# A load order, a moved norm and a new order of the first rows in a two-batch transformer kernel

## The chip, the cores and the metric

The kernel runs on one core of one Trainium2 chip. A core has a matrix engine (TensorE, PE in the profile; its weight loads are PEld), a vector engine (VectorE, DVE), a scalar engine (ScalarE, ACT), GpSimd (POOL) and SyncE (SP), which here issues nearly all DMAs. Each engine works through its own instructions in the order written and waits on semaphores. The metric is the device time of one execution in microseconds (us); lower is better.

## The reference

Two layers on x of 2 batches x 2048 rows x 512 features, all in float32. The part that matters here is the first: x is normalised, goes through single-head causal self-attention, and is added and normalised again. What follows (cross-attention to 77 context rows, a small MLP, a feed-forward layer of width 2048 with dequantised weights) isn't touched.

```python
def _layernorm(x, axis=-1, eps=1e-05):
    m = jnp.mean(x, axis=axis, keepdims=True)
    v = jnp.var(x, axis=axis, keepdims=True)
    return (x - m) / jnp.sqrt(v + eps)
...
    def self_attn(x, Wq, Wk, Wv):
        Q, K, V = (x @ Wq, x @ Wk, x @ Wv)
        energy = jnp.einsum('bqd,bkd->bqk', Q, K)
        lengths = jnp.sum(energy[:, 0] != 0, axis=-1)
...
        energy = jnp.where(pad | causal, NEG_INF, energy)
        score = jax.nn.softmax(energy / np.sqrt(DK), axis=-1)
        return jnp.einsum('bqk,bkd->bqd', score, V)
...
    z = self_attn(x, Wq1, Wk1, Wv1)
    x = layer_norm(x + z, ln1_g, ln1_b)
...
x = x + jnp.tanh(g_xattn[0]) * _L0_xattn_ref(_layernorm(x, axis=-1), ctx_1024, ...)
```

## The kernel before

**Precision.** Every product is made of three passes on float32 values split into a high and a low half (`PASSES`). So each result that feeds another product is read out of its bank (PSUM) twice: ScalarE copies the high half (`hi`, L1009) and VectorE subtracts it to get the low half (`lo`, L1494). A product of four chunks is 12 matmuls (`product`, L643). Turns (transposes) by PE are at L653 and L687, those of the attention's probabilities at L777.

**Stages.** A prologue (0 to about 65 us) turns and joins the weights. Then each batch has an x stage and an attention stage; batch 0 ends and batch 1 starts at about 365 to 405 us; the attention of batch 1 ends at about 730 us. The rest of the 1749 us isn't touched.

**The x stage** goes over 16 tiles of 128 rows. For tile t: SP loads it into one of four places (`load_xa`, L397; place t % 4 is free when tile t-4 has been normed), VectorE makes mean and variance (`stats_x`, L1528 and L1530), GpSimd the reciprocal root (`rstd_x`, L1330 and L1332), VectorE the norm (`norm_x`, L1553) into one of two places, PE turns it (`turn_x`, L653), ScalarE and VectorE split it (`hi_x`, `lo_x`) into xT, PE multiplies it with the value weights (`values`), and these are split too (`hi_v`, `lo_v`). VectorE also makes the dot of the normed tile with the first query (`dot_x`, L1571), whose non-zero results are the key count. PE's order is values(t-2), turn_x(t), values(t-1), turn_x(t+1) and so on. Tiles 0 to 2 are done ahead: in batch 0 in the prologue, in batch 1 inside the last row of batch 0's attention.

**The attention stage** goes over 16 rows i of 128 queries; row i has i // 4 + 1 chunks of keys. Its order is written out by hand in `attention_order`, as triples (kind, i, c), and every engine walks the same list and does its own part of each entry:

- S: scores of row i, chunk c (PE; VectorE masks them and takes the maximum, L1658 and L1668). X: exponentials (ScalarE, L1077).
- T: turn the probabilities (PE L777, ScalarE hi, VectorE lo). V: product with the values (PE).
- Q: a chunk of the next four rows' queries (PE, hi, lo).
- A: the end of a row, first part: VectorE norms that row's x again, divides and adds (L1681 to L1686), makes statistics (L1528, L1530); GpSimd makes the root, and then `make_xo(i + 2)` (L1351), a sum with the loaded rows of x that waits for their DMA. B: second part, VectorE scales and shifts (L1534, L1536); then SP stores the row (L495) and loads the x of row i + 2 (`load_x`, L471), and stores what `make_xo` made (L475).
- In the last row of batch 0 (15): L statistics, M norm, N turn and split of tiles 0 to 3 of batch 1, W the split of the value weights, D the product for the first query. VectorE's norm of tile 0 of batch 1 goes into the place from which `make_xo` reads a bias row (`b3_row`), so it waits until the last `make_xo` of batch 0 is made.

**SP's queue** is one list in order. In batch 0's prologue the loads of tiles 0 to 3 and of the value weights are followed by two stores (g_scratch 640 KB, v_scratch 616 KB, L464 and L466) which wait for the last product of the prologue, and then by the loads of tiles 4 and on. Between the batches the first four tiles of batch 1 are asked for after the last store of `make_xo`'s results; they lie where the scores of even rows lie (`Srow`), so they wait until row 14's probabilities are turned.

**Before the first scores** PE makes queries(0, m) for four chunks m, with the one-column product that counts the keys (L758) ahead of chunk 2. VectorE makes all four low halves, then reads the count (L1632), builds the padding mask (L1638 to L1644), and only then releases the banks for scores. PE waits for all four low halves before row 0's scores.

## Time and profile before

| what | value |
|---|---|
| time, median of 3 runs | 1750.45 us (1750.41 to 1756.3) |
| profiled execution, its own time | 1750.76 us |
| its span, first to last instruction | 1749.0 us |
| PE busy | 1667.6 us (95%) |
| VectorE busy | 847.7 us (48%) |
| ScalarE busy | 550.6 us (31%) |
| GpSimd busy | 359.5 us (21%) |
| chain that ended last: PE, VectorE, ScalarE, DMA, GpSimd, issue | 82%, 8%, 2%, 2%, 2%, 2% |
| mean granted TensorE clock | 0.981 of full speed |

The profile is one execution, taken by the hardware profiler. A share of busy time is an average over stages with different limits, so the stages that the change touches have to be read one by one: where an engine sat idle, for how long, and what released it. Matmuls are pipelined and their ends are modelled, so rows of PE may overlap by some tenths of a microsecond. TensorE's clock is granted at one of two levels, 1.2 or 2.4 GHz; 1.00 in a window means all of it at 2.4, 0.5 all of it at 1.2. Times in the rows are from the start of the span.

### The profile page before, as it was taken

The page shows a single profiled execution, that of the slowest core. Times are in us where ns is not written, and L with a number is a line of the kernel's source. Part 1 is how long each engine was busy: PE and PEld are TensorE (multiplying, and loading weights), DVE is VectorE, ACT ScalarE, POOL GpSimd, SP SyncE. Part 2 cuts the span into 40 slices and gives each one's busy share as a digit, 9 for nine tenths or more (in the row PEclk, how much of TensorE's full clock was granted, in tenths as well). Part 3 has the DMA queues.
Part 4 walks back from the last instruction along what each step waited for, and adds up shares of the span by engine and source line. Part 5 has one row for each costly group of instructions (what it writes and reads, how often), then busy time and mean ns, then how long its engine had stood idle before and what let it go on. Part 6 is the DMA issues. An engine that isn't in the chain of part 4 may idle for free.

```text
span 1749.0 us, 20563 instructions
## 1 busy us (share of the span) xinstructions
PE 1667.6 (95%) x7734; PEld 1355.9 (78%) x7734; DVE 847.7 (48%) x1746; ACT 550.6 (31%) x964; POOL 359.5 (21%) x509
## 2 busy tenths in 40 slices
PE   6998999989999999889999799999999999999999
PEld 4777888866778888668778587878787887878787
DVE  4576653448564534578788765322323223232311
ACT  3222211112211212266656534222223223232222
POOL 0121110112121100078888830100000000000000
PEclk9999999989999999799999899999999999999999
DMA  6211211122021101734544342101010101000000
GB/s 188 72 49 65 74 37 37 37 72 91 19 85 43 55 30 37 243 105 157 181 151 150 126 134 84 61 0 49 1 49 0 49 0 49 1 26 23 6 20 24
DMA packets 68822, 117.22 MB, mean 67 GB/s; under 512 B 11201, under 2 KB 13249, under 8 KB 68571
## 3 DMA queue, kind: packets, MB, share of 16 engines
q1 hardware_dynamic: 64968, 110.12, 19.1%
q10 hardware_dynamic: 3757, 5.80, 1.1%
q8 instruction: 62, 1.02, 0.2%
q14 instruction: 35, 0.29, 0.1%
HBM read 81.05 MB, written 34.84 MB: 66 GB/s over the span
## 4 chain that ended last, share of the span: by engine, by line
PE 82%; DVE 8%; ACT 2%; DMA 2%; POOL 2%; issue 2%; SPq 0%; ACTq 0%; DVEq 0%; POOLq 0%
PE banks L643 77%; PE banks L653 3%; PE banks L777 2%; DMA plain<-in_x 1%; DVE split_q L1494 1%; ACT split_q L1009 1%; DVE plain L1997 1%; ACT split L1009 1%; DVE split L1962 1%; DVE split L1494 1%; DVE plain L2040 1%; DVE small L1528 1%; DMA plain<-in_L_xattn_Wq 1%; DMA plain<-in_L_xattn_fc_w 0%; DVE plain L1571 0%
## 5 line engine op out<-in xcount | busy, mean ns | idle before, releaser
L643 PE MATMUL banks<-split_q,split 128*128 128x512 f32 x2328 | 576.8, 397 | 5.6 <-POOL split L1387 4.5
L643 PE MATMUL banks<-split 128*128 128x512 f32 (+4 forms) x2292 | 551.5, 391 | 28.3 <-DVE split L1494 16.0
L643 PEld LDWEIGHTS banks<-split 128*128 128x128 f32 (+3 forms) x2292 | 417.3, 188 | 131.8 <-issue 22.8
L643 PEld LDWEIGHTS banks<-split_q,split 128*128 128x128 f32 x2328 | 434.6, 190 | 99.2 <-POOL split L1387 6.1
L643 PE MATMUL banks<-split,split_q 128*128 128x512 f32 (+2 forms) x1728 | 396.0, 382 | 5.2 <-DVE small L1632 3.5
L643 PEld LDWEIGHTS banks<-split,split_q 128*128 128x128 f32 x1728 | 307.6, 190 | 61.5 <-DVE split_q L1494 4.3
L1494 DVE TENSOR_TENSOR split<-banks,split 128x512 fp32r<-128x512 f32 (+5 forms) x232 | 146.8, 641 | 173.3 <-ACT split L1009 172.7
L1009 ACT ACTIVATE split<-banks 128x512 fp32r<-128x512 f32 (+5 forms) x232 | 125.8, 557 | 323.9 <-PE banks L777 198.4
L1962 DVE TENSOR_TENSOR split<-plain,split 128x512 fp32r<-128x512 f32 x128 | 88.3, 690 | 256.5 <-ACT split L1300 256.4
L1294 ACT ACTIVATE plain<-banks,small 128x512 f32<-128x512 f32 x128 | 87.7, 685 | 285.9 <-PE banks L643 285.9
L1494 DVE TENSOR_TENSOR split_q<-banks,split_q 128x512 fp32r<-128x512 f32 x68 | 46.8, 688 | 254.4 <-ACT split_q L1009 254.4
L1009 ACT ACTIVATE split_q<-banks 128x512 fp32r<-128x512 f32 x68 | 40.5, 598 | 298.8 <-PE banks L653 205.2
L643 PE MATMUL banks<-split_x,split 128*128 128x512 f32 x444 | 109.1, 394 | 3.5 <-DVE split L1962 3.5
L1413 POOL TENSOR_TENSOR small<-small 128x4 f32<-128x4 f32 x8 | 2.1, 264 | 498.5 <-DVE small L1981 498.5
L643 PEld LDWEIGHTS banks<-split_x,split 128*128 128x128 f32 x444 | 82.2, 188 | 25.6 <-DVE split L1962 8.8
L1351 POOL TENSOR_TENSOR plain<-plain 128x512 f32<-128x512 f32 x32 | 41.2, 1288 | 287.5 <-DMA plain<-in_x 283.1
L653 PE MATMUL banks<-ident,plain 128*128 128x128 f32 x432 | 69.6, 295 | 29.0 <-DMA plain<-in_L_xattn_Wq 11.2
L653 PEld LDWEIGHTS banks<-ident,plain 128*128 128x128 f32 x432 | 54.7, 151 | 48.2 <-DVE plain L1553 15.6
L1300 ACT ACTIVATE split<-plain 128x512 fp32r<-128x512 f32 x128 | 81.0, 633 | 4.1
L1330 POOL TENSOR_TENSOR small<-small 128x1 f32<-128x1 f32 x64 | 18.4, 287 | 294.5 <-DVE small L1530 294.1
L1077 ACT ACTIVATE plain<-plain,small 128x128 f32<-128x128 f32 (+15 forms) x32 | 38.6, 1206 | 111.6 <-DVE small L1674 111.6
L1658 DVE CUSTOM_DVE_ANT_0 plain<-banks,plain 128x512 f32<-128x512 f32 (+2 forms) x72 | 43.4, 602 | 59.4 <-PE banks L643 58.5
(151 smaller groups left out, 1244.4 us busy)
## 6 DMA issues: line engine op xcount, KB each, us to landing
...
```

Source lines behind the costliest of these rows:

```text
L643: mm = nc.tensor.matmul(out, left(c, l), right(c, r), start=start and c == 0 and (l, r) == PASSES[0], stop=stop and c == chunks - 1 and (l ...
L653: mm = nc.tensor.transpose(bank[:, c * P:(c + 1) * P], block_of(c), ident[:])
L777: mm = nc.tensor.transpose(PS[:, 2 + n % 2, j * P:(j + 1) * P], Srow[:, i % 2, lo:lo + P], ident[:])
L1009: nc.scalar.activation(dst, src, copy).then_inc(sems[1], inc)
L1077: nc.scalar.activation(Srow[:, i % 2, 0:w], Srow[:, i % 2, 0:w], ACT.Exp, bias=nb[:, i % 2:i % 2 + 1], scale=SCALE, accum_out=rowsum[:, i ...
L1294: nc.scalar.activation(HF3[:, f % 2], PS[:, f % 2], ACT.Silu, bias=b1f[:, f:f + 1]).then_inc(hf3_ready, 1)
L1300: nc.scalar.activation(hid3[f % 2][:, 0, :], HF3[:, f % 2], copy).then_inc(f_hi, 1)
L1330: nc.gpsimd.tensor_tensor(out, var, eps_col, ALU.add).then_inc(eps_added, 1)
L1351: nc.gpsimd.tensor_tensor(x_shifted, xin[:, i % 2], b3_row, ALU.add).then_inc(xo_made, 1)
L1494: nc.vector.tensor_tensor(dst, src, hi_part.bitcast(F32), ALU.subtract).then_inc(sems[1], inc)
L1658: return nc.vector.tensor_tensor_reduce(out=row[:, at + lo_:at + lo_ + n], in0=src, in1=pad[:, at + lo_:at + lo_ + n], scale=1.0, scalar=- ...
L1962: nc.vector.tensor_tensor(hid3[f % 2][:, 1, :], HF3[:, f % 2], hid3[f % 2][:, 0, :].bitcast(F32), ALU.subtract).then_inc(f_lo, 1)
```

## The change

1. **Loads, batch 0.** SP asks for tiles 4, 5 and 6 right behind the value weights, each when tile t-4 is normed, ahead of the two stores. The later loop begins at tile 7.
2. **Loads, batch 1.** The first four tiles are asked for one row earlier (at i = 13, before the wait for row 13's end), tiles 4 to 6 at i = 15, before the wait for row 15's end. The value weights stay at i = 14.
3. **Norm of tiles 3 to 15.** It leaves VectorE. ScalarE makes it as an Identity with a scale (the reciprocal root) and a bias, minus mean times root; GpSimd makes the bias with two more operations on one column. In ScalarE's order it stands ahead of `hi_v(t - 2)`. It waits for the bias, the turn of tile t-2, the dot of tile t-2 and the norm of tile t-1.
4. **Before the first scores.** VectorE reads the count after two of the four low halves and spreads the rest over the mask's making. PE's first scores wait chunk by chunk (`first_score`).
5. **Order of rows 0 to 3.** Row 0's A is parted into Z (norm and add) and E (statistics, root, `make_xo`); Z comes ahead of row 2's turn, E and B behind it; B of row 0 is now behind V of row 2, B of row 1 behind Q's chunk 2, and row 3's exponentials behind row 2's turn.

```diff
@@ -89,9 +89,9 @@
 
 
     order = [("S", 0, 0), ("X", 0, 0), ("S", 1, 0), ("X", 1, 0), ("T", 0, 0), ("S", 2, 0), ("X", 2, 0), ("V", 0, 0),
-             ("T", 1, 0), ("S", 3, 0), ("X", 3, 0), ("A", 0, 0), ("V", 1, 0), ("B", 0, 0), ("T", 2, 0), ("Q", 1, 0),
-             ("A", 1, 0), ("V", 2, 0), ("Q", 1, 1), ("B", 1, 0), ("Q", 1, 2), ("A", 2, 0), ("Q", 1, 3), ("B", 2, 0),
-             ("T", 3, 0), ("S", 4, 0), ("S", 4, 1), ("X", 4, 0), ("V", 3, 0)]
+             ("T", 1, 0), ("S", 3, 0), ("Z", 0, 0), ("V", 1, 0), ("T", 2, 0), ("X", 3, 0), ("E", 0, 0), ("Q", 1, 0),
+             ("V", 2, 0), ("B", 0, 0), ("A", 1, 0), ("Q", 1, 1), ("Q", 1, 2), ("B", 1, 0), ("A", 2, 0), ("Q", 1, 3),
+             ("B", 2, 0), ("T", 3, 0), ("S", 4, 0), ("S", 4, 1), ("X", 4, 0), ("V", 3, 0)]
     for i in range(4, NB):
         n0 = chunks_of(i)
         n1 = chunks_of(i + 1) if i + 1 < NB else 0
...
@@ -153,7 +153,7 @@
     for b in range(B):
         order += [("x", b, t) for t in range(AHEAD + 2, NB)]
         for kind, i, c in ORDER:
-            if kind == "A":
+            if kind in ("A", "E"):
                 order.append(("z", b, i))
             elif kind == "L" and b + 1 < B:
                 order.append(("x", b + 1, c))
...
@@ -460,6 +461,9 @@
                              allow_slow_non_contiguous=True).then_inc(const_in, 16)
             sp.wait_ge(split_lo, C)
             weight("L0_xattn_Wv1", wv_raw[0], wv_in)
+            for t in range(4, 7):
+                sp.wait_ge(x_normed, t - 3)
+                load_xa(sp, 0, t)
             sp.wait_ge(mm_free, 2 + MM0)
             sp.dma_start(g_dram.rearrange("b p n -> p b n"),
                          g_0.rearrange("p b c h n -> p b (c h n)").bitcast(F32)).then_inc(parked, 16)
...
@@ -474,7 +478,7 @@
                     sp.wait_ge(xo_made, b * NB + i + 1)
                     sp.dma_start(xo_dram[b * S + i * P:b * S + (i + 1) * P, :], x_shifted).then_inc(xo_stored, 16)
 
-                for t in range(4, NB):
+                for t in range(7, NB):
                     sp.wait_ge(x_normed, b * NB + t - 3)
                     load_xa(sp, b, t)
                 load_x(0)
...
@@ -485,10 +489,15 @@
                 for i in range(NB):
                     if i + 1 < NB:
                         store_xo(i + 1)
-                    if i == NB - 2 and b + 1 < B:
+                    if i == NB - 3 and b + 1 < B:
                         sp.wait_ge(tp_full, TURNS["p", b, NB - 2, 3] + 1)
                         for t in range(4):
                             load_xa(sp, b + 1, t)
+                    if i == NB - 1 and b + 1 < B:
+                        for t in range(4, 7):
+                            sp.wait_ge(x_normed, (b + 1) * NB + t - 3)
+                            load_xa(sp, b + 1, t)
+                    if i == NB - 2 and b + 1 < B:
                         sp.wait_ge(s_full, (b + 1) * SS1)
                         weight("L0_xattn_Wv1", wv_raw[1], wv_in)
                     sp.wait_ge(x1_ready, b * NB + i + 1)
...
@@ -757,11 +766,10 @@
                         pe.wait_ge(counted, b + 1)
                         nc.tensor.matmul(PS[:, 0, 0:1], all_ones, keys_seen, start=True, stop=True).then_inc(s_full, 2)
                     queries(0, m)
-                pe.wait_ge(mm_free, b * MM1 + 2 + MM0 + NB + C)
 
                 for kind, i, c in ORDER:
                     if kind == "S":
-                        if i % 4 == 0 and c == 0 and i:
+                        if i % 4 == 0 and c == 0:
                             first_score(2 + T_BEFORE[i], i // 4, 0, width_of(i, 0))
                         else:
                             score(2 + T_BEFORE[i] + c, i % 4, c * 512, width_of(i, c))
...
@@ -1054,6 +1062,14 @@
                     "p (b n) -> p b n", b=B), sems=(mm_full, mm_hi))
 
 
+            def norm_x(b, t):
+                act.wait_ge(mean_scaled, 2 * (b * (NB - AHEAD - 1) + t - AHEAD))
+                act.wait_ge(tp_full, TURNS["x", b, t - 2, 0] + 1)
+                act.wait_ge(dotted, b * NB + t - 1)
+                act.wait_ge(x_normed, b * NB + t)
+                nc.scalar.activation(xn[:, t % 2], xa[:, t % 4], ACT.Identity, bias=nmr1[:, t:t + 1],
+                                     scale=rs1[:, t:t + 1]).then_inc(x_normed, 1)
+
             for b in range(B):
                 def hi_v(t):
                     hi(MM0 + t, V[t][:, 0, :], PS[:, 4 + t % 2], b, MM1, (mm_full, mm_hi))
...
@@ -1062,6 +1078,8 @@
                     hi(MM0 + NB + g * C + m, QT[:, m, 0, :], PS[:, 4 + m % 2], b, MM1, (mm_full, mm_hi))
 
                 for t in range(AHEAD, NB):
+                    if t > AHEAD:
+                        norm_x(b, t)
                     if t - AHEAD == 4:
                         act.wait_ge(parked, 32)
                     hi_v(t - AHEAD)
...
@@ -1333,6 +1352,14 @@
 
             def rstd_x(b, t):
                 rstd(NORMS["x", b, t], mv1[:, t, 1:2], rs1[:, t:t + 1])
+                if t > AHEAD:
+                    n = b * (NB - AHEAD - 1) + t - AHEAD
+                    pool.wait_ge(rstd_ready, NORMS["x", b, t] + 1)
+                    nc.gpsimd.tensor_tensor(nmr1[:, t:t + 1], mv1[:, t, 0:1], rs1[:, t:t + 1], ALU.mult).then_inc(
+                        mean_scaled, 1)
+                    pool.wait_ge(mean_scaled, 2 * n - 1)
+                    nc.gpsimd.tensor_tensor(nmr1[:, t:t + 1], zero_col, nmr1[:, t:t + 1], ALU.subtract).then_inc(
+                        mean_scaled, 1)
 
             for t in range(AHEAD + 2):
                 rstd_x(0, t)
...
@@ -1353,7 +1380,7 @@
                 make_xo(0)
                 make_xo(1)
                 for kind, i, c in ORDER:
-                    if kind == "A":
+                    if kind in ("A", "E"):
                         rstd(NORMS["z", b, i], mvE[:, i % 2, 1:2], rsE[:, i % 2:i % 2 + 1])
                         if i + 2 < NB:
                             make_xo(i + 2)
...
@@ -1615,8 +1642,6 @@
                 for t in range(AHEAD, NB + AHEAD):
                     if AHEAD + 2 <= t + 1 < NB:
                         stats_x(b, t + 1)
-                    if AHEAD + 1 <= t < NB:
-                        norm_x(b, t)
                     if AHEAD <= t - 1 < NB:
                         lo_x(b, t - 1)
                     lo_v(t - AHEAD)
...
@@ -1624,9 +1649,8 @@
                         dot_x(b, t - 1)
                 nc.vector.tensor_scalar(cnt16, row_0, 0.0, None, ALU.not_equal, ALU.add,
                                         accum_out=keys_seen).then_inc(counted, 1)
-                for m in range(C):
-                    lo_q(0, m)
-
+                lo_q(0, 0)
+                lo_q(0, 1)
                 dve.wait_ge(s_full, b * SS1 + 2)
                 for c in range(4):
                     ins = nc.vector.tensor_scalar(lnc[:, c:c + 1], PS[:, 0, 0:1], -512.0 * c, None, ALU.add)
...
@@ -1637,11 +1661,12 @@
                 for c in range(4):
                     last = p1.done(nc.vector.tensor_scalar(pad[:, c * 512:(c + 1) * 512], keys[:],
                                                            lnc[:, c:c + 1], -BIG, ALU.is_ge, ALU.mult))
+                lo_q(0, 2)
                 p1.wait(last)
-
                 p1.link(nc.vector.reciprocal(ln, lnc[:, 0:1]))
                 p1.link(nc.vector.tensor_scalar(ln, ln, 0.0, None, ALU.mult))
                 p1.link(nc.vector.tensor_scalar(pad, pad, ln, None, ALU.add))
+                lo_q(0, 3)
 
                 def scores(i, c):
                     k, w, at = 2 + T_BEFORE[i] + c, width_of(i, c), c * 512
...
@@ -1674,7 +1699,7 @@
                     nc.vector.tensor_scalar(nb[:, i % 2:i % 2 + 1], nmx[:, 0:1], -SCALE, None,
                                             ALU.mult).then_inc(mx_ready, 1)
 
-                def end_a(i):
+                def add_rows(i):
 
                     dve.wait_ge(x_in[i % 2], b * NB * 8 + (i // 2 + 1) * 16)
                     dve.wait_ge(xo_made, b * NB + i + 1)
...
@@ -1686,6 +1711,8 @@
                     nc.vector.scalar_tensor_tensor(out=U[:, i % 2], in0=PS[:, 6 + i % 2],
                                                    scalar=rcp[:, i % 2:i % 2 + 1], in1=xin[:, i % 2],
                                                    op0=ALU.mult, op1=ALU.add).then_inc(z_free, 1)
+
+                def stats_z(i):
                     dve.wait_ge(z_free, b * NB + 2 + i + 1)
                     statistics(p1, U[:, i % 2], mvE[:, i % 2], i + 1)
...
@@ -1703,7 +1730,12 @@
                         n, k, w = TURNS["p", b, i, c], T_BEFORE[i] + c, width_of(i, c)
                         lo(n, PT[k % 2][:, 1, 0:w], PS[:, 2 + n % 2, 0:w], PT[k % 2][:, 0, 0:w])
                     elif kind == "A":
-                        end_a(i)
+                        add_rows(i)
+                        stats_z(i)
+                    elif kind == "Z":
+                        add_rows(i)
+                    elif kind == "E":
+                        stats_z(i)
                     elif kind == "B":
                         end_b(i)
                     elif b + 1 < B and kind == "L":
...
```

In the `x` stage of batch 0, ScalarE's order (names: banks is PSUM, split is xT and V, plain is a float32 area with x as loaded, normed x and scores; L1009 and L1017 are `hi`, L1070 is the new norm). Before:

```order
L1009 ACTIVATE split<-banks 128x512
L1009 ACTIVATE split<-banks 128x4x128
L1009 ACTIVATE split<-banks 128x512
L1009 ACTIVATE split<-banks 128x4x128
L1009 ACTIVATE split<-banks 128x512
```

and after:

```order
L1017 ACTIVATE split<-banks 128x512
L1017 ACTIVATE split<-banks 128x4x128
L1070 ACTIVATE plain<-plain,small 128x512
L1017 ACTIVATE split<-banks 128x512
L1017 ACTIVATE split<-banks 128x4x128
L1070 ACTIVATE plain<-plain,small 128x512
```

A third operation per tile stands between the split of one tile and the values of the next.

SP's queue at the end of batch 0 (L471 and L475 load x of a row, L475 and L479 store what `make_xo` made, L397 and L398 load tiles of batch 1, L438 and L439 the value weights, L495 and L504 store a row). Before:

```order
L495 DMA x_scratch<-plain 128x512
L471 DMA plain<-in_x 128x512
L475 DMA xo_scratch<-plain 128x512
L397 DMA plain<-in_x 128x512 x4
L438 DMA raw<-in_L_xattn_Wv 128x4x512
L495 DMA x_scratch<-plain 128x512 x2
L397 DMA plain<-in_x 128x512 x12
```

and after:

```order
L398 DMA plain<-in_x 128x512 x4
L504 DMA x_scratch<-plain 128x512
L475 DMA plain<-in_x 128x512
L479 DMA xo_scratch<-plain 128x512
L439 DMA raw<-in_L_xattn_Wv 128x4x512
L504 DMA x_scratch<-plain 128x512
L398 DMA plain<-in_x 128x512 x3
L504 DMA x_scratch<-plain 128x512
L398 DMA plain<-in_x 128x512 x9
```

The four loads moved ahead of row 13's store, row 15's load and the store behind it, and three of the next twelve ahead of row 15's store.

VectorE's order in attention rows 0 to 2 of batch 0, from row 0's division and sum on (L1686 and L1711). Before:

```order
L1686 SCALAR_TENSOR_TENSOR plain<-banks,small,plain 128x512
L1528 BN_STATS small<-plain 128x6
L1530 BN_AGGR small<-small 128x2
L1534 SCALAR_TENSOR_TENSOR plain<-plain,small 128x512
L1536 SCALAR_TENSOR_TENSOR plain<-plain,small 128x512
L1494 TENSOR_TENSOR split<-banks,split 128x384
L1494 TENSOR_TENSOR split_q<-banks,split_q 128x512
```

and after:

```order
L1711 SCALAR_TENSOR_TENSOR plain<-banks,small,plain 128x512
L1521 TENSOR_TENSOR split<-banks,split 128x384
L1555 BN_STATS small<-plain 128x6
L1557 BN_AGGR small<-small 128x2
L1521 TENSOR_TENSOR split_q<-banks,split_q 128x512
L1561 SCALAR_TENSOR_TENSOR plain<-plain,small 128x512
L1563 SCALAR_TENSOR_TENSOR plain<-plain,small 128x512
```

The low half of row 2's turned probabilities (128x384) now comes right behind the sum, and row 0's end behind the first chunk of the next queries.

## Rows read from the trace of the kernel before

**Rows 1.** The page: busy us, share of the span, instructions

```profile
PE 1667.6 (95%) x7734; PEld 1355.9 (78%) x7734; DVE 847.7 (48%) x1746; ACT 550.6 (31%) x964; POOL 359.5 (21%) x509
```

**Rows 2.** Windows: stretch, us, busy of each engine (x instructions), clock, DMA, GB/s

```profile
70.00:80.00 10.00, 7.55 (x27) 6.19 (x28) 6.15 (x13) 1.68 (x3) 1.97 (x4) 0.66 0.28 88
```

**Rows 3.** Timeline of PE, batch 0: start, us, line, [idle before <- releaser]

```profile
72.45 1.12 PE L653 MATMUL banks<-ident,plain 128*128 128x128 f32 x4 [3.96 <-DVE plain L1553]
...
78.11 0.60 PE L653 MATMUL banks<-ident,plain 128*128 128x128 f32 x4
...
114.41 0.60 PE L653 MATMUL banks<-ident,plain 128*128 128x128 f32 x4
...
117.74 0.60 PE L653 MATMUL banks<-ident,plain 128*128 128x128 f32 x4
```

**Rows 4.** Timeline of all engines, the same place: VectorE

```profile
66.62 0.68 DVE L1571 SCALAR_TENSOR_TENSOR plain<-banks,plain 128x512 f32<-128x512 f32 x1
...
70.90 0.69 DVE L1528 BATCH_NORM_STATS2 small<-plain 128x6 f32<-128x512 f32 x1 [3.59 <-DMA plain<-in_x]
```

**Rows 5.** Timeline of all engines, one tile of batch 1's x stage

```profile
407.57 0.69 DVE L1494 TENSOR_TENSOR split<-banks,split 128x512 fp32r<-128x512 f32 x1 [0.43 <-ACT split L1009]
...
408.91 0.69 DVE L1528 BATCH_NORM_STATS2 small<-plain 128x6 f32<-128x512 f32 x1
...
409.85 0.55 DVE L1553 TENSOR_SCALAR plain<-plain,small 128x512 f32<-128x512 f32 x1
...
410.31 1.30 DVE L1494 TENSOR_TENSOR split<-banks,split 128x512 fp32r<-128x512 f32 x2
...
410.45 0.66 PE L653 MATMUL banks<-ident,plain 128*128 128x128 f32 x4 [0.20 <-DVE plain L1553]
```

**Rows 6.** Groups by form: ScalarE over the span, GpSimd at 75 to 118

```profile
L1171 ACT ACTIVATE plain<-plain,small 128x512 f32<-128x512 f32 x28 | 22.7, 812 | 16.0 <-DVE plain L1997 16.0
...
L1332 POOL TENSOR_TENSOR small<-small 128x1 f32<-128x1 f32 x11 | 6.0, 549 | 0.9
L1330 POOL TENSOR_TENSOR small<-small 128x1 f32<-128x1 f32 x11 | 4.5, 414 | 30.4 <-DVE small L1530 30.4
```

**Rows 7.** Timeline of all engines between the batches

```profile
358.93 0.49 PE L777 MATMUL banks<-ident,plain 128*128 128x128 f32 x3
...
367.47 1.09 ACT L1009 ACTIVATE split<-banks 128x512 fp32r<-128x512 f32 x2 [1.33 <-PE banks L777]
368.61 1.26 POOL L1351 TENSOR_TENSOR plain<-plain 128x512 f32<-128x512 f32 x1 [19.44 <-DMA plain<-in_x]
...
370.26 1.87 SPq L397 DMA_DIRECT2D plain<-in_x  x4
...
373.05 0.69 DVE L1528 BATCH_NORM_STATS2 small<-plain 128x6 f32<-128x512 f32 x1 [7.60 <-DMA plain<-in_x]
...
374.15 0.19 POOL L1330 TENSOR_TENSOR small<-small 128x1 f32<-128x1 f32 x1 [4.29 <-DVE small L1530]
...
375.70 5.46 PE L643 MATMUL banks<-split 128*128 128x512 f32 x12 [7.89 <-DVE split L1494]
```

**Rows 8.** Timeline of PE, batch 1's x stage: turns of tiles 3 and 14

```profile
403.27 0.66 PE L653 MATMUL banks<-ident,plain 128*128 128x128 f32 x4 [3.24 <-DVE plain L1553]
...
442.72 0.60 PE L653 MATMUL banks<-ident,plain 128*128 128x128 f32 x4
```

**Rows 9.** Timeline, attention rows 0 to 3; the last row is of batch 1

```profile
136.71 3.00 PE L643 MATMUL banks<-split,split_q 128*128 128x128 f32 x24 [1.77 <-DVE small L1632]
...
154.10 2.29 PE L643 MATMUL banks<-split 128*128 128x512 f32 x9 [2.88 <-DVE split L1494]
...
160.39 0.74 DVE L1534 SCALAR_TENSOR_TENSOR plain<-plain,small 128x512 f32<-128x512 f32 x1
...
169.55 2.98 PE L643 MATMUL banks<-split 128*128 128x512 f32 x12 [0.49 <-DVE split L1494]
...
483.05 3.51 PE L643 MATMUL banks<-split 128*128 128x512 f32 x9 [2.89 <-DVE split L1494]
```

4 lines of the change are left out of this document (3 added, 1 removed).

## The prediction

> **What bounds the kernel now.** I read the page's busy times first: TensorE (PE) is busy for 95% of the span [rows 1]. So what an edit to VectorE, ScalarE or a load is worth is only the time in which PE waits for them. The table by windows shows where that is in the part that the diff touches: at 70 to 80 us, for one, PE is busy for 7.55 of 10 us, with a granted clock of 0.66 [rows 2]. The timelines of these places give four kinds of loss:
>
> 1. At 68.49 to 72.45, in the first tiles of batch 0, PE waits 3.96 us for the norm of tile 3 [rows 3]. VectorE stands in front of it with the statistics of tile 4, which wait for their load until 70.90 [rows 4]: that load was queued on SP behind two large stores.
> 2. In the rest of the x stage two tiles take 7.18 us (403.27 to 410.45), 3.59 each [rows 5, 8], while PE alone needs 3.33 (114.41 to 117.74) [rows 3].
> 3. Between the batches PE waits 7.89 us (to 375.70), then runs 12 products in 5.46 us that elsewhere take 2.98, and waits again 3.24 us before 403.27 [rows 7 to 9].
> 4. In the first four rows of attention it waits 1.77, 2.88 and 0.49 us [rows 9].
>
> **The change part by part.**
>
> Early loads, batch 0. Tiles 4 to 6 are now asked for as soon as the norms of tiles 0 to 2 are made, ahead of the two stores. Tile 2 is normed before tile 3, so all three are there long before 70.90. VectorE can begin tile 4's statistics when the dot of tile 1 is done (66.62 + 0.76 = 67.4 [rows 4]). ScalarE's norm of tile 3 waits for the same dot and takes 0.81 us [rows 6], to 68.2; PE wants it at 68.49. The low half of tile 2 comes after the statistics (408.91 to 409.85 in [rows 5], 0.94) and ends at 69.1, so PE's next values start some 0.2 late. Tile 4's turn stood at 78.11 and should stand at 68.49 + 3.33 + 0.2 = 72.0: **6.1 us less**. 2.3 us of that is the slow clock after the wait (from 72.45 to 78.11 one tile took 5.66 us, not 3.33 [rows 3]).
>
> Norm on ScalarE. Before, one chain ran twice per pair of tiles: the product ends, ScalarE copies 0.6, VectorE makes the low half (407.57), the dot, the statistics, and the norm (409.85), and PE turns it at 410.45 [rows 5]. The norm leaves VectorE, 0.45 us from start to start of a neighbour. What replaces it: ScalarE waits for the dot (about 2.1 us after a product's end), norms in 0.81 [rows 6] and is ready at 2.95, while PE comes for it at 3.33: 0.4 us of slack. ScalarE's load rises to 0.6 + 0.6 + 0.81 = 2.0 of 3.33 us. GpSimd gets two one-column operations a tile. The nearest row is its add, 0.41 us on average here and 0.19 in the one at 374.15 [rows 6, 7]; with the power, 0.55 [rows 6], the bias is ready 1.3 to 2.1 us after the statistics, which run a tile ahead, so it comes before the dot or with it. Next late is VectorE's low half of x: 410.31 + 0.69 before, 0.45 earlier now, within 0.1 us of where PE wants it. So I take 3.36 us a tile. Batch 0, tiles 4 to 14: 36.30 us (78.11 to 114.41 [rows 3]) become 33.6, **2.7 less**. Batch 1, tiles 3 to 14: 39.45 (403.27 to 442.72 [rows 8]) become 37.0, **2.4 less**.
>
> One rule speaks on GpSimd's share. The row shows the add at 0.41 us on average in the x stage, where it starts within VectorE's norm, and 0.19 us where it starts beside a statistics instruction [rows 6, 7]. The Trainium skill, page "SBUF — State Buffer", section "Who interferes with whom", says that GpSimd and VectorE share one pair of ports, that a tensor_scalar of VectorE may take the pair whole, and that the other then blocks for the instruction. By that rule the three short operations cost 0.19 each once the norm has left VectorE, and the bias has 0.8 us of slack instead of none; the sum above is the same by either, the chance of the rival on ScalarE is not.
>
> Between the batches. The next batch's first four tiles are now loaded one row earlier. Their place in memory is free when row 14's last scores are turned, at 359.4; before, SP asked for them only at 370.26, because it stood behind row 13's store, the load of row 15 and the store that needs it [rows 7]. Of that step all moves: four loads; the weights stay where they were and are asked for at 370.3, 1.9 us earlier. VectorE comes free at 373.05 - 7.60 = 365.45 and makes two statistics by 367.3; ScalarE has row 15's first transposes evicted at 368.05 [rows 7], VectorE's low half ends at 368.7, and PE starts at 368.9 instead of 375.70: **6.8 less**. With a wait of 1.0 us in place of 7.89 the slow clock goes too: 5.46 - 2.98 [rows 7, 9], **2.5 less**. What is late next: the norm of tile 0 overwrites what GpSimd reads until 369.9 (368.61 + 1.26 [rows 7]), and GpSimd's roots follow, so it is made at 371.3, when PE is still in its first product (to 371.8). Two further waits of 0.2 to 0.3 us appear behind VectorE's row end, so **0.5 back**. Before 403.27 the second load wait goes (tiles 4 to 6 are asked for before row 15's store), but ScalarE's norm of tile 3 and the low half of tile 2 are still behind the dot: 3.24 us become about 1.0, **2.2 less**. Together 11.0.
>
> First groups. Counting the keys moves ahead of the last two low halves and the first scores may start on three of four chunks, so the 1.77 us become 0.4. Row 0's statistics and end move behind rows 2 and 3, so the third product, at 154.10 [rows 9], can start at about 149.7. But little of these 4.4 us survives. Row 1's end stood at 160.39 [rows 9]; now it is queued behind Q's third chunk, whose low half ends at 159.0: 1.4 us earlier. From there the chain is unchanged: SP's load of row 3, GpSimd's sum with it, the root of row 2, row 2's end, the low half, PE at 169.55. So the last product of the group starts **1.4 us earlier per batch**, 2.8 together, and PE waits some 2.2 us there in place of 0.49. Bounds: 0 (the chain starts no earlier) to 4.4 a batch (it binds nothing).
>
> Sum: 6.1 + 2.7 + 2.4 + 11.0 + 2.8 = 25.0. The profiled execution took 1750.76 us for a span of 1749.0; the median of the runs is 1750.45. **Forecast 1725.5 us.**
>
> **The rivals.**
> - *Clock.* In batch 1 the wait of 2.89 us was followed by 9 products in 3.51 us, in batch 0 the same wait by 9 in 2.29 [rows 9]. The new 2.2 us wait may draw the slow clock in either batch (1.2 us each and as much again behind it), or the old losses may go. The Trainium skill, "TensorE: Matmul & The Clock Gate", Part 1, says that the monitor runs freely, not from the wait's start; by that rule neither case can be read off the length of a wait, and the two rows agree. Price: minus 2 to plus 4.5, 1723 to 1730; inside the forecast's own range.
> - *First groups pay in full.* If row 1's end is not held by the chunk's low half, up to 3 us more a batch: 1719.5.
> - *A new wait between the batches.* VectorE does rows' ends and the next batch's tiles in one order; if tile 0's norm (held by GpSimd to 371.3) keeps PE from its second product, half of the 11.0 stays lost: 1731. If the loads come no earlier, since SP still waits somewhere before them (the change doesn't do what it says), all 11: 1736.5.
> - *ScalarE's chain leads, and the kernel gets slower.* The new norm stands ahead of the copy of the values on ScalarE. This closes a loop without PE: norm 0.81, copy 0.6, low half 0.6, dot 0.75, together 2.8 us a tile. It decides from 3.33. The other parts gain 19.9, so slower than before by 0.5% needs a loop of 3.59 + (19.9 + 8.8) / 23 = 4.8 us. That would take a table load (1.28 us each way) around each Identity: loop 5.4, time 1750.8 - 19.9 + 23 x 1.8 = 1772. Against it: Identity already runs beside Exp and Copy in the cross stage at 0.81 us [rows 6], and the built program still has three table loads.
> - A milder form: the bias or the dot comes 0.3 us late, and the pace stays at 3.59: 1730.6.
>
> **How the numbers follow.** Half a per cent (8.8 us) is about what a measurement of this kernel can tell from no change. Forecast with its clock cases, 1720 to 1730.5: 0.62. First groups in full, 1714 to 1720: 0.11. Pace unchanged or half of the gain between the batches lost, 1730.5 to 1735: 0.16. Loads no earlier, 1735 to 1741: 0.06. Within 0.5%: 0.02. Slower: 0.03. The range 1717 to 1734 leaves out less than 2 in 10. Faster 0.95.
>
> **What would show it.** Right: no wait at 68.49; turns in the x stage 3.33 to 3.4 us apart; SP's four loads of tiles at about 359; PE's first product of row 15 at 368.9 less the 10.2 us gained before it, in 3.0 us; in both first groups a wait of 2 us before the last product. Wrong: turns still 3.59 apart with ScalarE or GpSimd named as releaser; a wait over 2 us behind row 15's first product; the last product of a first group 4 us earlier, not 1.4. The sum is most exposed in the part between the batches, which carries 11 of 25 us on a chain that no row shows as a whole.

## The result, and the profile after

| | before | after |
|---|---|---|
| first measurement, median of 4 runs each | 1753.38 us (1750.41 to 1759.38) | 1726.08 us (1724.2 to 1726.23) |
| the same kernel after once more, beside 9 runs of before | 1752.96 us (1749.56 to 1757.45) | 1724.9 us (1723.93 to 1726.59) |
| profiled execution, span | 1749.0 us | 1724.2 us |

The ratio is 0.9838 with an interval of 0.9806 to 0.9869, and 0.9839 (0.982 to 0.9857) the second time: faster by 1.6%. The forecast was 1725.5 us, 25.0 less than before. The medians of the two comparisons differ by 27.3 and 28.1 us, the two profiled executions by 24.7 (24.8 of span). One execution, the profiled one of the experiment "Loads alone", ran throughout at a mean granted clock of 0.576 and took 2680.52 us; it stands in no number below.

The page of the changed kernel: span, busy us with share and instructions, and the chain that ended last.

```profile
span 1724.2 us, 20645 instructions
...
PE 1658.7 (96%) x7734; PEld 1351.6 (78%) x7734; DVE 836.8 (49%) x1720; ACT 570.2 (33%) x990; POOL 362.4 (21%) x562
...
PE 86%; DVE 6%; ACT 2%; POOL 2%; DMA 2%; issue 1%; ACTq 0%; SPq 0%; DVEq 0%
```

Against [rows 1] the 26 norms have gone from DVE to ACT (1746 to 1720 and 964 to 990 instructions), and POOL has its operations on one column. PE's busy time fell by 8.9 us with the same 7734 matmuls, which fits slow clock that went. The rest of the 24.8 us of span is idle time of PE.

Windows of the kernel after (us, busy of each engine, clock, DMA share, GB/s), the stretch of [rows 2]:

```profile
70.00:80.00 10.00, 10.00 (x50) 7.95 (x49) 7.90 (x19) 5.48 (x9) 3.37 (x12) 1.00 0.29 79
```

PE is busy for 10.00 instead of 7.55 us, with 50 matmuls instead of 27 and a granted clock of 1.00 instead of 0.66. The timeline of PE in batch 0's x stage, where [rows 3] had its turns (start us, us, line, idle before and releaser):

```profile
67.53 0.66 PE L662 MATMUL banks<-ident,plain 128*128 128x128 f32 x4
...
71.05 0.60 PE L662 MATMUL banks<-ident,plain 128*128 128x128 f32 x4
...
104.56 0.60 PE L662 MATMUL banks<-ident,plain 128*128 128x128 f32 x4
```

The turn of tile 3 has no wait. From tile 3's turn to tile 4's it is 3.52 us, one tile plus the 0.2 us of the late low half, and the ten tiles to 104.56 take 33.51 us, 3.35 each.

The timeline between the batches and at the end of batch 1's x stage (SPq is SP issuing a DMA), where [rows 7, 8] were:

```profile
348.86 1.76 SPq L398 DMA_DIRECT2D plain<-in_x  x4
```

```profile
358.35 2.98 PE L652 MATMUL banks<-split 128*128 128x512 f32 x12 [1.13 <-DVE split L1521]
...
365.21 0.63 PE L662 MATMUL banks<-ident,plain 128*128 128x128 f32 x4 [0.28 <-DVE split L1521]
...
381.25 0.66 PE L662 MATMUL banks<-ident,plain 128*128 128x128 f32 x4 [0.72 <-ACT plain L1070]
...
418.27 0.60 PE L662 MATMUL banks<-ident,plain 128*128 128x128 f32 x4
```

The wait of 7.89 us is 1.13, the product behind it takes 2.98 instead of 5.46, and the wait of 3.24 is 0.72. The eleven tiles take 37.02 us.

One tile of batch 1 on all engines, the counterpart of [rows 5]:

```profile
386.20 0.68 DVE L1598 SCALAR_TENSOR_TENSOR plain<-banks,plain 128x512 f32<-128x512 f32 x1
...
386.92 0.70 DVE L1555 BATCH_NORM_STATS2 small<-plain 128x6 f32<-128x512 f32 x1
387.06 0.82 ACT L1070 ACTIVATE plain<-plain,small 128x512 f32<-128x512 f32 x1 [1.01 <-DVE plain L1598]
...
387.86 0.66 DVE L1521 TENSOR_TENSOR split<-banks,split 128x512 fp32r<-128x512 f32 x1
...
387.97 0.62 PE L662 MATMUL banks<-ident,plain 128*128 128x128 f32 x4
388.02 0.19 POOL L1349 TENSOR_TENSOR small<-small 128x1 f32<-128x1 f32 x1 [2.48 <-DVE small L1557]
...
388.29 0.55 POOL L1351 TENSOR_TENSOR small<-small 128x1 f32<-128x1 f32 x1
...
388.92 0.19 POOL L1358 TENSOR_TENSOR plain<-small 128x1 f32<-128x1 f32 x1
```

The norm on ACT starts at the end of the dot (387.06) beside VectorE's statistics of the next tile, takes 0.82 us to 387.88, and PE turns its result at 387.97. GpSimd's add takes 0.19 us here, where [rows 6] had a mean of 0.41.

The first groups of attention, PE of batch 0 and then of batch 1:

```profile
113.69 1.52 PE L652 MATMUL banks<-split,split_q 128*128 128x512 f32 x6
...
139.50 2.20 PE L652 MATMUL banks<-split 128*128 128x512 f32 x9
...
152.95 2.27 PE L652 MATMUL banks<-split,split_q 128*128 128x512 f32 x15 [0.56 <-DVE split_q L1521]
...
157.40 4.58 PE L652 MATMUL banks<-split 128*128 128x512 f32 x12 [2.19 <-DVE split L1521]
...
161.80 0.61 PE L785 MATMUL banks<-ident,plain 128*128 128x128 f32 x4
...
427.57 1.75 PE L652 MATMUL banks<-split,split_q 128*128 128x512 f32 x7
...
471.33 4.54 PE L652 MATMUL banks<-split 128*128 128x512 f32 x12 [2.25 <-DVE split L1521]
```

The product of 9 has lost its wait of 2.88 us, and the last product of the group has a wait of 2.19 in place of 0.49 [rows 9]. Those 12 matmuls then take 4.58 and 4.54 us, not 2.98; the granted clock over them is 0.62 and 0.63 (157.40 to 161.90, 471.33 to 475.70). The same three places (first queries, last product, next turn) in the kernel before, of which [rows 9] has only the product: the queries of batch 0 and 1 and the turns behind the products.

```profile
123.65 1.52 PE L643 MATMUL banks<-split,split_q 128*128 128x512 f32 x6
...
172.37 0.60 PE L777 MATMUL banks<-ident,plain 128*128 128x128 f32 x4
...
451.99 1.30 PE L643 MATMUL banks<-split,split_q 128*128 128x512 f32 x5
...
502.88 0.60 PE L777 MATMUL banks<-ident,plain 128*128 128x128 f32 x4
```

From these and from [rows 3, 7 to 9] comes the account of the 24.8 us of span. Where 358.93 stood before, the same turns stand at 348.35; batch 1's last product started at 500.06 before, and the turn behind it stands at 475.68 after.

| stretch | before | after | gained | predicted |
|---|---|---|---|---|
| start to tile 2's turn (not touched) | 65.11 | 64.28 | 0.8 | 0 |
| to tile 4's turn | 13.00 | 6.77 | 6.2 | 6.1 |
| batch 0, tiles 4 to 14 | 36.30 | 33.51 | 2.8 | 2.7 |
| first queries to the last product of the group | 45.90 | 43.71 | 2.2 | 1.4 |
| that product, to the next turn | 2.82 | 4.40 | -1.6 | 0 |
| rest of batch 0's attention (172.37 to 358.93) | 186.56 | 186.55 | 0 | 0 |
| between the batches (358.93 to 403.27) | 44.34 | 32.90 | 11.4 | 11.0 |
| batch 1, tiles 3 to 14 | 39.45 | 37.02 | 2.4 | 2.4 |
| first queries to the last product, batch 1 | 48.07 | 43.76 | 4.3 | 1.4 |
| that product, to the next turn | 2.82 | 4.35 | -1.5 | 0 |
| all behind it (not touched) | 1246.1 | 1248.5 | -2.4 | 0 |

Tile 14's turn to the first queries gives 0.1 more. The last line is code that no edit touches, and it changes from one execution to the next: in the second measurement's profiled execution (1723.93 us) it took 1245.35 us, and over all the profiled executions here, "Loads alone" left out, 1245.3 to 1250.3.

### The profile page after: what moved, and what is told of

The parts are those of the page before. It is cut to its first block, busy times and chain, and to the rows that moved or that the text cites. A ratio compares the mean times of both kernels' runs of the same rounds, so it can differ in the third digit from the quotient of the medians.

```text
span 1724.2 us, 20645 instructions
## 1 busy us (share of the span) xinstructions
PE 1658.7 (96%) x7734; PEld 1351.6 (78%) x7734; DVE 836.8 (49%) x1720; ACT 570.2 (33%) x990; POOL 362.4 (21%) x562
## 3 DMA queue, kind: packets, MB, share of 16 engines
q8 instruction: 62, 1.02, 0.2%
## 4 chain that ended last, share of the span: by engine, by line
PE 86%; DVE 6%; ACT 2%; POOL 2%; DMA 2%; issue 1%; ACTq 0%; SPq 0%; DVEq 0%
PE banks L652 80%; PE banks L662 3%; PE banks L785 2%; DVE split_q L1521 1%; ACT split_q L1017 1%; DVE plain L2029 1%; DVE split L1994 1%; DVE plain L2072 1%; DVE split L1521 1%; DMA plain<-in_L_xattn_Wq 1%; DMA plain<-in_L_xattn_fc_w 1%; DMA plain<-in_x 0%; ACT split L1017 0%; POOL split L1414 0%; POOL plain L1426 0%
## 5 line engine op out<-in xcount | busy, mean ns | idle before, releaser
L1017 ACT ACTIVATE split<-banks 128x512 fp32r<-128x512 f32 (+5 forms) x232 | 124.7, 557 | 268.1 <-PE banks L785 207.6
L1017 ACT ACTIVATE split_q<-banks 128x512 fp32r<-128x512 f32 x68 | 40.5, 598 | 290.9 <-PE banks L662 205.4
L1378 POOL TENSOR_TENSOR plain<-plain 128x512 f32<-128x512 f32 x32 | 41.3, 1291 | 284.3 <-DMA plain<-in_x 279.8
L1349 POOL TENSOR_TENSOR small<-small 128x1 f32<-128x1 f32 x64 | 12.8, 199 | 263.7 <-DVE small L1557 263.1
```

What stands on the lines that cost most here:

```text
L1017: nc.scalar.activation(dst, src, copy).then_inc(sems[1], inc)
L1378: nc.gpsimd.tensor_tensor(x_shifted, xin[:, i % 2], b3_row, ALU.add).then_inc(xo_made, 1)
```

## Experiments

Each was timed beside runs of the kernel before (medians 1751.19, 1751.1 and 1752.96 us in the three sets). "Control" is the kernel after in the last set, 1724.9 us.

### One part of the change at a time

**Loads alone**: only the edits to SP's order (points 1 and 2 of the change) in the kernel before.

> The kernel before with the new load order of SP alone (parts 1 and 2 of the change). My theory, by the sum of the prediction: batch 0 loses its wait of 3.96 us for the first tile but keeps VectorE's norm behind the statistics, so 5.5 us less with the slow clock; between the batches the 7.89 us wait, the slow clock and the 3.24 us wait go, 11 us less; the pace of the x stage stays at 3.59 us a tile. Together 16.5 us, 1734. Rival (the loads only work together with the norm on ScalarE, because VectorE's one order is what holds the tiles): the waits before tile 3's turn stay near 3 us and the gain is under 10 us, above 1740.

Measured: 1735.9 us (1734.07 to 1739.9, three runs), ratio 0.9903 (0.9873 to 0.9932). That is 15.3 us less, the size that was expected, and the interval leaves out the rival's "under 10 us". Where in the kernel these 15.3 us fall, no trace shows.

**Norm alone**: only point 3.

> The kernel before with the norm of tiles 3 to 15 on ScalarE and its bias on GpSimd alone (part 3). My theory: the pace of the x stage falls from 3.59 to 3.36 us a tile, which is 5.1 us less over both batches, and the load waits stay (VectorE's low half of tile 2 still stands behind tile 4's statistics): 1745. GpSimd's add falls from 0.41 to 0.19 us in the x stage. Rival (without early loads ScalarE's chain, not VectorE's, sets the pace): pace 3.59 or more, 1750 or above.

Measured: 1745.93 us (1743.12 to 1749.96, eight runs), ratio 0.9963 (0.9947 to 0.9979), 5.3 us less. PE at tile 3 of batch 0:

```profile
71.41 5.49 PE L644 MATMUL banks<-split_q,split 128*128 128x512 f32 x12 [3.60 <-DVE split L1515]
```

The turn of tile 3 has no wait any more, but the wait went to the product behind it, with the slow clock, because VectorE's low half still stands behind the statistics that wait for the load. Ten tiles (80.03 to 113.39) took 33.36 us: the pace of 3.34 comes from the norm alone and needs nothing else. GpSimd's add has a mean of 0.19 us here too (75 to 118 us), as expected, so its 0.41 went with VectorE's norm and not with the loads.

**First groups alone**: only points 4 and 5.

> The kernel before with the new order before and in the first four rows alone (parts 4 and 5). My theory: the last product of the group starts 1.4 to 2.2 us earlier per batch, and a wait of 2.2 us before it may draw the slow clock, so between 0 and 4.5 us less in all: 1748. Rival (the whole 4.4 us at the third product survives): 1741 to 1742.

Measured: 1749.99 us (1745.66 to 1752.82, ten runs), ratio 0.9983 (0.9968 to 0.9999), 1.2 us less. The last product of batch 0's group:

```profile
167.76 3.00 PE L643 MATMUL banks<-split 128*128 128x512 f32 x12 [2.50 <-DVE split L1492]
```

It starts 1.8 us earlier than at 169.55 [rows 9], though 2.88 us of waiting went ahead of it: the waits ahead came back as 2.50 here. Both first groups with their last products are 4.9 us shorter in this trace (1.9 and 3.1), while the span is only 2.1 less: the untouched stretches behind them took 0.9 and 1.8 us more. So the median's 1.2 us may be too little for this part; its interval reaches 5.6. The three parts add up to 21.8 us, the whole has 27.3 and 28.1. Some of the gap may be what two parts do only together, as at tile 3, but the loads' interval alone is 10 us wide, so I don't divide it further.

### One part taken away from the whole

**Batch 1's first tiles asked for at i = 14 again**, all else as after:

```diff
-                    if i == NB - 3 and b + 1 < B:
-                        sp.wait_ge(tp_full, TURNS["p", b, NB - 2, 3] + 1)
-                        for t in range(4):
-                            load_xa(sp, b + 1, t)
...
                     if i == NB - 2 and b + 1 < B:
+                        sp.wait_ge(tp_full, TURNS["p", b, NB - 2, 3] + 1)
+                        for t in range(4):
+                            load_xa(sp, b + 1, t)
```

> The changed kernel with the first four tiles of batch 1 asked for where they were before, after the last store of the sums (tiles 4 to 6 stay early). My theory: the wait of 7.9 us before row 15's first product returns with the slow clock behind it, 8.8 us more: 1735. Rival (the wait alone, without a slow clock): 6.8 us more, 1733. Rival (VectorE's row end or GpSimd holds this place anyway): under 3 us more.

Measured: 1732.93 us (1730.91 to 1734.71), ratio 0.9894 (0.9879 to 0.9909): 8.0 more than the control, 6.9 more than the first measurement.

```profile
366.57 5.21 PE L651 MATMUL banks<-split 128*128 128x512 f32 x12 [8.01 <-DVE split L1520]
```

Wait and slow clock of [rows 7] are back together (granted clock 0.53 from 366.57 to 371.60). The product starts 8.2 us later than at 358.35, and the turn of tile 3, at 391.21, stands 10.0 behind 381.25. But 1.3 us of both were there before the loads matter: the turns of 348.35 stand at 349.68 in this execution. From them to the turn of tile 3 it is 41.53 us, 8.6 more than the 32.90 of the kernel after (8.8 expected). So the four loads carry 8.6 of the 11.4 us of that step; the rest stays with tiles 4 to 6, which are still early here, and the norm.

**Batch 0's tiles 4 to 6 behind the two stores again** (`range(7 if b else 4, NB)`, and the early loop out):

> The changed kernel with tiles 4 to 6 of batch 0 asked for behind the two stores, as before. My theory: VectorE's low half of tile 2 stands behind tile 4's statistics again, PE waits 3.4 us and more before the values of tile 2 and runs at the slow clock after it: 5 to 6 us more, 1731.5. Rival (with the norm on ScalarE the late load no longer matters): under 1 us more.

Measured: 1729.94 us (1726.85 to 1730.12), ratio 0.9873 (0.9858 to 0.9888): 3.9 to 5.0 more.

```profile
72.55 5.38 PE L649 MATMUL banks<-split_q,split 128*128 128x512 f32 x12 [3.58 <-DVE split L1518]
...
77.77 0.60 PE L659 MATMUL banks<-ident,plain 128*128 128x128 f32 x4
```

From tile 2's turn (65.07 in this execution) to tile 4's it is 12.70 us, 5.9 more than the 6.77 of the kernel after. Further on this execution ran the last product of batch 0's group in 2.99 us after a wait of 2.18, where the kernel after took 4.58, so 1.6 came back.

### How much slack the norm on ScalarE has

A second Identity of the same size, into an unused bank, ahead of the norm:

```diff
                 act.wait_ge(x_normed, b * NB + t)
+                nc.scalar.activation(PS[:, 7], xa[:, t % 4], ACT.Identity, bias=nmr1[:, t:t + 1],
+                                     scale=rs1[:, t:t + 1])
```

> The changed kernel with a second Identity of 128x512 on ScalarE (to an unused bank) between the wait for the dot and the norm, 0.8 us more on its chain for each of 26 tiles. My theory: 0.4 us of slack takes half of it, the turn of a tile comes 0.4 us late, and since the delay is felt once per two tiles the pace goes from 3.36 to about 3.55: 4 to 5 us more, 1730. Rival A (no slack, ScalarE's norm already sets the pace): 0.8 a tile, 19 us more, 1745. Rival B (the norm is hidden altogether): no change, 1726.

Measured: 1731.5 us (1729.81 to 1733.29), ratio 0.9883 (0.9866 to 0.9899), 5.4 to 6.6 more. Timeline at tile 3:

```profile
66.58 0.78 ACT L1070 ACTIVATE banks<-plain,small 128x512 f32<-128x512 f32 x1 [1.09 <-DVE plain L1600]
67.30 0.80 ACT L1072 ACTIVATE plain<-plain,small 128x512 f32<-128x512 f32 x1
...
68.15 0.66 PE L662 MATMUL banks<-ident,plain 128*128 128x128 f32 x4 [0.58 <-ACT plain L1072]
```

The second instruction adds 0.72 us, and twelve tiles take 42.96 us (68.15 to 111.11), 3.58 each: 0.23 us a tile over 3.35. With 23 tiles that is 5.3 us, as measured. The size is the expected one, the way to it isn't: the delay was to be felt once per two tiles. Four tiles further on the rows show what sets the pace:

```profile
81.07 0.78 ACT L1070 ACTIVATE banks<-plain,small 128x512 f32<-128x512 f32 x1 [0.70 <-DVE plain L1600]
...
81.79 0.80 ACT L1072 ACTIVATE plain<-plain,small 128x512 f32<-128x512 f32 x1
...
82.52 0.60 ACT L1017 ACTIVATE split<-banks 128x512 fp32r<-128x512 f32 x1
...
83.15 0.69 DVE L1523 TENSOR_TENSOR split<-banks,split 128x512 fp32r<-128x512 f32 x1 [0.62 <-ACT split L1017]
...
83.76 0.68 DVE L1600 SCALAR_TENSOR_TENSOR plain<-banks,plain 128x512 f32<-128x512 f32 x1
...
84.62 0.78 ACT L1070 ACTIVATE banks<-plain,small 128x512 f32<-128x512 f32 x1 [0.69 <-DVE plain L1600]
```

Norm, copy of the values, their low half, dot, and the next norm follow each other, each released by the one before, 3.55 us from 81.07 to 84.62. This is the loop without PE that the prediction had among its rivals, at 2.8 us a tile: with 0.72 more it is 3.5 and leads. In the kernel after it has about 0.5 us of slack a tile (3.35 less 2.83, which is 3.55 less 0.72).

### What holds the last product of the first group

The chain in the kernel after: GpSimd's sum for row 3 (L1378) waits for that row's load and stands ahead of row 2's root (L1349, L1351), and VectorE's end of row 2 (L1561) waits for the root.

```profile
153.01 1.29 POOL L1378 TENSOR_TENSOR plain<-plain 128x512 f32<-128x512 f32 x1 [5.36 <-DMA plain<-in_x]
...
155.12 0.75 DVE L1561 SCALAR_TENSOR_TENSOR plain<-plain,small 128x512 f32<-128x512 f32 x1 [2.22 <-POOL small L1351]
```

**One row later**, GpSimd's sums: the root first, the sum for the next row behind it.

```diff
-                        if i + 2 < NB:
+                        if 0 < i < 4:
+                            make_xo(i + 1)
+                        if 2 < i < NB - 2:
                             make_xo(i + 2)
```

> The changed kernel with one edit: in rows 1 to 3 GpSimd makes the sum with the loaded rows of x one row later, so that the root of a row no longer stands behind a load that waits for the row before. My theory (the chain end of row 1, load of row 3, GpSimd's sum, root of row 2, end of row 2, low half, product is what eats the first groups' gain): the waits of 2.19 and 2.25 us before the last product of the group go to under 0.5, the product runs in 2.9 us and not 4.6, and the time falls by 3 to 7 us against the changed kernel, to 1719 to 1723. Rival (VectorE's own load of work in these rows is the limit): the waits stay above 1.5 us and the time stays at 1726.

Measured: 1722.73 us (1722.21 to 1723.91), ratio 0.9824 (0.9803 to 0.9845). The time is in the range, the wait isn't. All engines there:

```profile
153.99 1.29 POOL L1378 TENSOR_TENSOR plain<-plain 128x512 f32<-128x512 f32 x1
...
154.06 1.77 DVE L1563 SCALAR_TENSOR_TENSOR plain<-plain,small 128x512 f32<-128x512 f32 x1 [0.36 <-POOL small L1351]
...
157.36 2.96 PE L652 MATMUL banks<-split 128*128 128x512 f32 x12 [1.35 <-DVE split L1523]
```

The root is in time now, but VectorE's instruction takes 1.77 us instead of 0.75: GpSimd's sum began 0.07 us ahead of it. In batch 1 it is the same, 1.77 at 465.74 behind a sum that began at 465.67. The wait only fell to 1.35. By its rows the two groups with their last products are 4.9 us shorter than in the kernel after; of that the medians show 3.4 against the first measurement and 2.2 against the control. The Trainium skill, page "SBUF — State Buffer", section "Who interferes with whom", says that a VectorE instruction with two inputs from SBUF contends with a GpSimd instruction that reads SBUF. The row agrees.

**The sums where VectorE isn't at a row's end**: row 2's sum stays one row later, row 3's waits until row 2's end is made, and rows 4 and 5 follow.

```diff
-                        if i + 2 < NB:
+                        if i == 1:
+                            make_xo(2)
+                        elif i == 3:
+                            make_xo(4)
+                            make_xo(5)
+                        elif 3 < i < NB - 2:
                             make_xo(i + 2)
+                    elif kind == "B" and i == 2:
+                        pool.wait_ge(x1_ready, b * NB + 3)
+                        make_xo(3)
```

> As e4_pool_later, but GpSimd makes the sum for row 3 only when VectorE has finished row 2's end. In e4 the two ran together and VectorE's first instruction of that end took 1.77 us instead of 0.74. My theory (the two engines block each other there): the instruction takes 0.75 again, the last wait of the group falls from 1.35 to 0.3 us, and the time is 1.0 us a batch less than e4's 1722.7, about 1721. Rival (the 1.77 is a chance of that execution or the wait's reading): the wait stays at 1.3 us, 1722.7.

Measured: **1717.17 us** (1716.36 to 1718.18), ratio 0.9794 (0.9775 to 0.9812).

```profile
153.87 0.75 DVE L1569 SCALAR_TENSOR_TENSOR plain<-plain,small 128x512 f32<-128x512 f32 x1 [0.35 <-POOL small L1351]
...
155.49 1.27 POOL L1378 TENSOR_TENSOR plain<-plain 128x512 f32<-128x512 f32 x1 [1.65 <-DVE plain L1571]
...
156.16 3.00 PE L652 MATMUL banks<-split 128*128 128x512 f32 x12 [0.33 <-DVE split L1529]
```

Apart from each other the same instruction takes 0.75 us, and the wait is 0.33 (also in batch 1). That GpSimd's sum holds VectorE's instruction up is shown so; that it happens at a port, as that page of the Trainium skill has it, no run here can tell from another way. Against "One row later" the rows show the 1.0 us a batch that was expected. The median fell by 5.6 us; 2.75 of the 4.9 between the two profiled executions lie in the untouched stretch behind the last first group, and the rest of the surplus is open. Against the control the gain is 7.7 us: 2.1 of waiting and 1.6 of slow clock in each batch make 7.4. This version is faster than both kernels.

**Row 1's end ahead of Q's chunk 2**, `("B", 1, 0)` and `("Q", 1, 2)` changed places in the order of the kernel after:

> The changed kernel with row 1's end (B) ahead of the third chunk of the next queries, as in the kernel before. My theory (row 1's end is held only by that chunk's low half): the end starts about 1.2 us earlier, and so does the last product of the group in each batch: 2 to 2.5 us less, 1724, if the wait of the third chunk's low half behind it holds nobody. Rival (the end is held by its root on GpSimd): no change.

Measured: 1722.36 us (1720.45 to 1724.12), ratio 0.9834 (0.9819 to 0.9848).

```profile
148.97 0.75 DVE L1561 SCALAR_TENSOR_TENSOR plain<-plain,small 128x512 f32<-128x512 f32 x1 [2.00 <-POOL small L1351]
...
158.15 2.98 PE L652 MATMUL banks<-split 128*128 128x512 f32 x12 [1.79 <-DVE split L1521]
```

The product starts only 0.4 us earlier after the queries than in the kernel after (43.28 against 43.71), not 1.2. Row 1's end starts 0.6 us earlier (34.10 against 34.73 behind the first queries) and then waits for its root on GpSimd: this is the rival, and it sets in after 0.6 us. Against the control the time is 2.5 us less, but the ratio to before is that of the kernel after (0.9838 and 0.9839), so the gain isn't clear of noise. This execution had no slow clock in batch 0, which is 1.6 us of one trace.

**Both of the last two edits:**

> As e9_pool_apart, with row 1's end also ahead of the third chunk of the next queries (e8's edit). My theory: with the root no longer behind a load, the order of VectorE is what is left; rows 1 and 2 end 1 us earlier, the waits of 0.56 and of the last product both go, no slow clock is drawn: 1718.5 to 1720.5. Rival (PE's own work is the limit after e9): same as e9 within 0.5 us.

Measured: 1717.6 us (1714.57 to 1718.88), ratio 0.9792 (0.9772 to 0.9811), the same as the sums apart by themselves, which is what the rival said. The rows are those of the theory: the product of 24 before the last one has no wait and the last one 0.21, and it starts 1.0 us a batch earlier after the queries (40.89 against 41.85). This doesn't show in runs that spread over 4 us; the untouched stretch behind took 2.1 us more in this execution. And the two engines meet again, now at row 1's end:

```profile
146.79 1.29 POOL L1378 TENSOR_TENSOR plain<-plain 128x512 f32<-128x512 f32 x1
...
146.80 1.83 DVE L1569 SCALAR_TENSOR_TENSOR plain<-plain,small 128x512 f32<-128x512 f32 x1
```

In batch 1 it is 1.77 behind a sum that began 0.07 us earlier (456.65, 456.58). It costs VectorE 1.0 to 1.1 us a batch; with a wait of 0.2 us left before the last product, PE hardly feels it.

### What the slow clock costs there

Nine unused matmuls into an unused bank, ahead of the last product of each first group, fill PE's wait:

```diff
+                        if i == 3:
+                            product(PS[:, 7], lambda m, h: QT[:, m, h, 0:P],
+                                    lambda m, h: xT[:, m, h, 0:512], 3)
                         pe.wait_ge(tp_free, 2 + TURNS["p", b, i, c] + 1)
```

> The changed kernel with nine matmuls (2.2 us) added on PE to a bank that is free, between row 4's scores and the last product of the first group, in both batches; their result isn't used. My theory (the wait of 2.2 us itself costs nothing more, the slow clock after it costs 1.6 us a batch and was drawn in both batches of the profiled execution): the product runs in 2.9 to 3.0 us and the time falls by 2 to 3 us where the slow clock was drawn, to 1722.5 to 1724. Rival (the clock falls for reasons other than this wait): no gain, or a loss of up to 0.5 us, 1725.5 to 1726.5.

and the kernel after beside it:

> The changed kernel once more, to stand beside the next three on one chip. All theories: 1724 to 1726.5.

Measured: 1723.15 us (1718.27 to 1723.92) and 1724.9 us (1723.93 to 1726.59). The last product of batch 0, first in the control, then with the filled wait:

```profile
158.06 4.58 PE L652 MATMUL banks<-split 128*128 128x512 f32 x12 [2.39 <-DVE split L1521]
```

```profile
158.14 3.00 PE L652 MATMUL banks<-split 128*128 128x512 f32 x12
```

Same work from within 0.1 us of the same start, 1.58 us less; the granted clock over the product is 0.61 in the control and 1.00 with the filled wait. In batch 1 a wait of 0.20 is left and the product takes 3.06 instead of 4.58. So in the trace the slow clock costs 1.5 to 1.6 us a batch. In the medians 1.75 of the 3.1 us appear, within ranges of 3 to 6 us. Two places at full speed wouldn't prove by themselves that filling the wait did it, since 4 of the 14 long waits in the table at the end were followed by full speed too; that none of the 12 places with a short or filled wait drew the slow clock supports it.

## Why the prediction was right, step by step

**Early loads, batch 0** (6.1 predicted, 6.2 measured). Right in each of its numbers: no wait at tile 3, the low half 0.2 us late, the slow clock gone. Taking these loads back puts tile 4's turn 5.9 us later. It also showed what the prediction said only in passing, that loads and norm need each other at this place: with the norm alone the wait moves to the product behind.

**Norm on ScalarE** (2.7 and 2.4 predicted, 2.8 and 2.4 measured). The pace is 3.35 and 3.37 us, 3.36 predicted. The mean is right, its make-up isn't. PE alone doesn't need 3.33: where nothing is late the turns stand 3.20 to 3.23 apart (71.05 to 74.25, 77.76 to 80.99), since the product follows its turn after 0.35 us and not after the 0.47 of the row read (114.41 to 114.88 in the kernel before). At every other tile it follows after 0.6 us (80.99 to 81.63), 0.05 behind the end of VectorE's low half of x (80.92 and 0.66), which stands behind the statistics. So PE alone was put 0.1 us a tile too high and the low half 0.1 too low, and the two cancel.

The slack of 0.4 us is found at every second turn in batch 0 (0.35 to 0.46); at the others ScalarE's norm ends only 0.05 to 0.10 ahead. What the added instruction measured is another slack, that of the loop without PE.

GpSimd's add fell from 0.41 to 0.19 us once VectorE's norm was gone, and the bias wasn't late: in one tile of each batch it was ready 0.83 and 1.52 us before its norm (82.44 to 83.27, 385.54 to 387.06). The Trainium skill, page "SBUF — State Buffer", section "Who interferes with whom", says that a tensor_scalar of VectorE can take the pair of ports that it shares with GpSimd, and that the one that comes second then blocks. The rows agree.

**Between the batches** (11.0 predicted, 11.4 measured). SP's four loads stand at 348.86; "about 359 less the shift of 10.2" is 348.8. PE's first product was predicted at 368.9 less the shift. The real shift at that point was 10.6 us (172.37 to 161.80, with the same 186.6 us behind it), which gives 358.3; it was 358.35, in 2.98 us. The two small waits were one of 0.28. The last wait became 0.72, not 1.0. These two make the 0.4 us that was too little.

**First groups** (1.4 a batch predicted). The mechanism is as predicted: a wait of 2 us before the last product takes the place of the old ones. But both sizes were off. The term was mis-sized at row 1's end: VectorE began it 34.73 us after the first queries (148.42 after 113.69) instead of 36.74 (160.39 [rows 9] after 123.65), 2.0 us earlier, and the product came 2.2 earlier. I had placed Q's low half 0.6 us too late. And the clock case that I had set beside the forecast, not into it, came in both batches: the last product took 1.6 us longer. Batch 0 netted 0.6 us. Batch 1 netted 2.8, because there an old loss went: the 9 products in 3.51 us [rows 9] now take 2.20, the 36 behind them 8.33 instead of 8.81, and 0.5 us more went at the first scores, where batch 1 had run at a granted clock of 0.72 (465.05 to 469.00) and batch 0 at 1.00. Together 3.4 us against 2.8: two errors of opposite sign.

**The price of the clock** was put at 1.2 us "and as much again". The new loss is 1.5 to 1.6 us in all, by the filled wait; the old one in batch 1 was 1.2 + 0.5 at the third and fourth row and 0.5 at the first scores, 2.2 in all (48.07 against 45.90 in batch 0).

**The rivals.** ScalarE's chain in the lead, the loads no earlier, the pace unchanged and the wait that moves between the batches all fell, by the rows above. First groups in full fell too: 2.2, not 4.4 us (batch 1's 4.3 has 2.2 of old slow clock in it). What the prediction missed is that the rest could be had: it named GpSimd's sum as a link in an unchanged chain, and moving the sums of rows 2 to 4 is worth 7.7 us.

The untouched parts gave 0.8 us at the start and took 2.4 at the end. The forecast was also counted from a median of 1750.45 us, and the runs of before that stand beside the result have 1753.38 and 1752.96: against them the gain is 27.3 and 28.1 us, not 25.0. So the agreement with 1725.5 to 0.6 us is partly luck; that of each step to 0.4 us, outside the first groups, isn't, though the pace is right by two errors that cancel.
